# A graph kernel's Y blocks copied out of PSUM in units of two banks and one

## The reference, cut to what matters

```python
h = maximum(layernorm(x), 0)
x = x + gnn(h, src, dst)                  # layer 0: segment sum of gathered rows
h = maximum(layernorm(x), 0)
for l in range(2):                        # layers 1 and 2
    msg  = h[src]
    agg  = segment_sum(msg, dst * 65 + type)
    mean = agg / maximum(count, 1)
    conv = einsum('nrd,rdk->nk', mean, W[l]) + h @ root[l] + bias[l]
    h    = relu(conv) + relu(h @ res_W[l] + res_b[l])
x = x + h
```

## Time and profile before

| | us |
|---|---|
| median of 3 runs | 13232.2 (13220.0 to 13239.15) |
| the profiled execution | 13350.5 |
| its span, first to last instruction | 13348.7 |
| ScalarE busy in the span | 2265.7 (17%) |
| TensorE busy (matmuls) | 5052.4 (38%) |
| VectorE busy | 5562.3 (42%) |
| GpSimd busy | 8102.8 (61%) |

### The profile page before, as it was taken

One profiled execution on the slowest core, in us unless ns is written; L12 is line 12 of the kernel. 1 busy time (PEld: TensorE's weight loads), 2 busy tenths in 40 slices (PEclk: granted clock), 3 DMA queues, 4 the chain that ended last, 5 costly groups with the idle time before them and its releaser, 6 DMA issues.

```text
span 13348.7 us, 141317 instructions
## 1 busy us (share of the span) xinstructions
PE 5052.4 (38%) x38979; PEld 3570.3 (27%) x39273; DVE 5562.3 (42%) x20233; ACT 2265.7 (17%) x5671; POOL 8102.8 (61%) x8294
## 2 busy tenths in 40 slices
PE   3556566666633333333333333322222222222222
PEld 3434444444422222222222222211111111111111
DVE  6754444444446556556565555611111111111111
ACT  4733333333311111111111111100000000000000
POOL 7355545555546666666666666566666666666666
PEclk5677777777765656666565566655555555555555
DMA  2122222222233333333333333311111111111111
GB/s 73 38 69 91 87 86 90 91 91 86 94 117 118 121 116 123 117 122 118 121 115 116 123 123 116 128 24 24 24 24 24 24 24 24 24 24 24 24 24 32
DMA packets 485430, 1012.61 MB, mean 76 GB/s; under 512 B 191444, under 2 KB 237540, under 8 KB 484548
## 3 DMA queue, kind: packets, MB, share of 16 engines
q1 hardware_dynamic: 227204, 742.28, 15.0%
q0 software_dynamic: 257920, 266.40, 10.4%
HBM read 558.25 MB, written 453.13 MB: 76 GB/s over the span
## 4 chain that ended last, share of the span: by engine, by line
another core or an unknown queue 43%; DVE 30%; issue 13%; PE 11%; ACT 2%; DVEq 1%; DMA 1%; SPq 0%; ACTq 0%; POOL 0%; POOLq 0%
DVE w_raw L1504 9%; DVE onehot L1496 5%; DVE w_parts L1496 5%; PE y_ps L1137 4%; DVE same_more L1504 4%; PE block_ps L1224 3%; DVE ystage L1459 2%; ACT scr L936 1%; PE y_ps L1216 1%; PE sums_ps L1189 1%; DMA y_table<-ystage 1%; PE signs_ps L1216 0%; ACT ystage L926 0%; DVE w_room L1510 0%
## 5 line engine op out<-in xcount | busy, mean ns | idle before, releaser
L798 POOL DMA_INDIRECT rows<-y_table,idx_st x3234 | 3054.0, 944 | 1866.5 <-issue 1094.1
L798 POOL DMA_INDIRECT w_parts<-y_table,idx_st x3212 | 3032.3, 944 | 1691.8 <-issue 951.4
L798 POOL DMA_INDIRECT rows<-h_table,idx_st x1452 | 1685.9, 1161 | 1372.4 <-PE sums_ps L1189 703.8
L1565 DVE TENSOR_SCALAR rr<-rr 128x64 f32<-128x64 f32 x198 | 39.4, 199 | 4552.9 <-remote 4474.7
L1137 PE MATMUL y_ps<-scr,hT 128*128 128x512 bf16 (+1 forms) x2574 | 825.0, 477 | 1877.5 <-ACT ystage L926 1174.4
L1327 PE MATMUL sums_ps<-onehot,rows 128*64 128x64 f32 x6468 | 832.4, 293 | 1819.5 <-issue 1517.4
L902 ACT ACTIVATE idx_st<-edges 128x11 int32 (+1 forms) x720 | 141.6, 211 | 8114.7 <-remote 7518.2
L1327 PE MATMUL sums_ps<-w_parts 128*64 128x64 f32 x6424 | 814.8, 290 | 1712.8 <-issue 1479.5
L926 ACT ACTIVATE ystage<-y_ps 128x512 f32<-128x512 f32 (+1 forms) x1782 | 994.3, 567 | 1574.1 <-PE y_ps L1137 841.4
L1327 PEld LDWEIGHTS sums_ps<-onehot,rows 128*64 128x64 f32 x6468 | 706.1, 202 | 1961.7 <-issue 1666.1
L1327 PEld LDWEIGHTS sums_ps<-w_parts 128*64 128x64 f32 x6424 | 690.5, 199 | 1863.5 <-issue 1588.0
(11 more groups left out here) (226 smaller groups left out, 7203.2 us busy)
## 6 DMA issues: line engine op xcount, KB each, us to landing
y_table<-ystage SPq DMA_DIRECT2D x396, 768.0 KB
edges<-key_row SPq DMA_DIRECT2D x198, 832.0 KB
y_table<-ystage SPq DMA_DIRECT2D x198, 608.0 KB
w_raw<-key_row SPq DMA_DIRECT2D x99, 832.0 KB
rows<-y_table,idx_st POOLq DMA_INDIRECT x3234
w_parts<-y_table,idx_st POOLq DMA_INDIRECT x3212
rows<-h_table,idx_st POOLq DMA_INDIRECT x1452
rr<-y_table SPq DMA_DIRECT2D x198, 64.0 KB, 1.8
```

What stands on the lines that cost most here:

```text
L798: pool.indirect_dma_start(out=rows_of(l, u)[:, j, k, 0:D], out_offset=None, in_=table, in_offset=bass.IndirectOffsetOnAxis(ap=idx_of(l, u, ...
```

## The change

Two neighbouring chunks that lie in one group now share one copy. A block's nine chunks become six units: (c0, c1), (c2), (c3, c4), (c5), (c6, c7), (c8). The two-chunk units go to `y_pair`, the two banks of `y_ps` under one name; the one-chunk units go to the first bank of `count_pair`, the two banks of `signs_ps` and `deg_ps`. All counters count units: TensorE raises `y_done` after the last chunk of a unit, and waits only before the first chunk of a unit, for the copy of the unit before the last one. The stores are as before: three a block, with the same bytes.

```diff
+    UNITS = [(g, c, min(c + 2, g * SG + SG, YC)) for g in range(YG) for c in range(g * SG, min(g * SG + SG, YC), 2)]
+    YP = len(UNITS)
+    UNIT_OF = [p for p, (g, c0, c1) in enumerate(UNITS) for c in range(c0, c1)]
...
-        y_ps = [pb(f"y_ps{i}") for i in range(2)]
+        y_pair = ctx.enter_context(nc.psum_tensor("y_ps", [P, 2 * BANK], f32))
+        y_ps = [y_pair[:, i * BANK:(i + 1) * BANK] for i in range(2)]
...
-        signs_ps = pb("signs_ps")
-        deg_ps = pb("deg_ps")
+        count_pair = ctx.enter_context(nc.psum_tensor("signs_ps", [P, 2 * BANK], f32))
+        signs_ps, deg_ps = (count_pair[:, i * BANK:(i + 1) * BANK] for i in range(2))
+        y_pairs = [y_pair, count_pair]
...
-                    wait_alone(sp, y_read[l], s * YC + min(g * SG + SG, YC) + 1)
+                    wait_alone(sp, y_read[l], s * YP + UNIT_OF[min(g * SG + SG, YC) - 1] + 2)
...
-                    for c in range(g * SG, min(g * SG + SG, YC)):
-                        act.wait_ge(y_done[l], s * YC + c + 1)
-                        o = (c - g * SG) * BANK
-                        nc.scalar.activation(ystage[:, n % 2, o:o + y_cols(c)],
-                                             y_ps[c % 2][:, 0:y_cols(c)], ACT.Copy).then_inc(y_read[l], 1)
+                    for p, (_, c0, c1) in enumerate(UNITS):
+                        if UNITS[p][0] == g:
+                            act.wait_ge(y_done[l], s * YP + p + 1)
+                            o, w = (c0 - g * SG) * BANK, min(c1 * BANK, YW) - c0 * BANK
+                            nc.scalar.activation(ystage[:, n % 2, o:o + w], y_pairs[p % 2][:, 0:w], ACT.Copy)\
+                              .then_inc(y_read[l], 1)
...
-                pe.wait_ge(y_read[l], s * YC + max(c - 1, 0) + 1)
+                p = UNIT_OF[c]
+                at = c - UNITS[p][1]
+                if at == 0:
+                    pe.wait_ge(y_read[l], s * YP + max(p - 1, 0) + 1)
...
-                ins.then_inc(y_done[l], 1)
+                if c + 1 == UNITS[p][2]:
+                    ins.then_inc(y_done[l], 1)
```

More of the change, by code:

```diff
@@ L1129, in transform_chunk @@
             def transform_chunk(l, s, c, v=0):
-                pe.wait_ge(y_read[l], s * YC + max(c - 1, 0) + 1)
+                p = UNIT_OF[c]
+                at = c - UNITS[p][1]
+                if at == 0:
+                    pe.wait_ge(y_read[l], s * YP + max(p - 1, 0) + 1)
                 n = y_cols(c)
                 lastc = c == YC - 1
+                to = y_pairs[p % 2][:, at * BANK:at * BANK + n]
                 for a in range(3):
-                    ins = nc.tensor.matmul(y_ps[c % 2][:, 0:n], hT[:, v, a // 2, :],
-                                           parts_of[l][:, a, c * BANK:c * BANK + n],
+                    ins = nc.tensor.matmul(to, hT[:, v, a // 2, :], parts_of[l][:, a, c * BANK:c * BANK + n],
                                            start=a == 0, stop=a == 2 and not lastc)
@@ L1141, in transform_chunk @@
                     o = R * D - c * BANK
-                    ins = nc.tensor.matmul(y_ps[c % 2][:, o:o + 2 * D], ones[:, :], brow[:, D:3 * D],
-                                           start=False, stop=True)
-                ins.then_inc(y_done[l], 1)
+                    ins = nc.tensor.matmul(to[:, o:o + 2 * D], ones[:, :], brow[:, D:3 * D], start=False, stop=True)
+                if c + 1 == UNITS[p][2]:
+                    ins.then_inc(y_done[l], 1)
             def transform(l, s, parts=range(YG)):
@@ L1259, in pe_turn @@
                     else:
-                        pe.wait_ge(y_read[0], n * YC - YC + 1)
+                        pe.wait_ge(y_read[0], n * YP - YP + 1)
                     count_chunk(m, 0)
```

## The result

| | before | after |
|---|---|---|
| median, us | 13234.5 (13220.0 to 13239.2) | 13394.0 (13385.0 to 13411.1) |
| runs | 4 | 4 |
| time as a ratio | 1 | 1.0125 (95% interval 1.0112 to 1.0137) |
| the profiled execution | 13350.5 | 13411.1 |

The change makes the kernel 1.25% slower, by about 160 us. The prediction said 13194 us, faster. The profiled execution of the kernel before took 116 us longer than the median of four and that of the changed kernel 17 us, so their difference (61 us) is not that of the kernels. I therefore took a second profile of the kernel before (experiment 8). It took 13241 us, as its median, and what follows compares with it where I say so. The record doesn't name the chip of the first comparison; that of the second profile has a median of 13240 us where the first had 13234, so differences of stage lengths between them may carry some microseconds of the chips.

The account below looks back on a forecast made before the run. No engine is full; TensorE's Y waits in stage one, held notices within gather runs, were the ceiling at 174 us. Gains of 30 + 6 + 2 + 0 = 38 us take 13232 to 13194 us, range 13120 to 13265.

Parts of the forecast that it names:

- So 0: Stage two: c8 leaves the line and copies end 1.0 us sooner, but other work covers this, so no gain.
- if the held notices move to other places in the turn: One listed sign that the prediction is wrong; notices had only been replayed with their old times.
- D: Rival, stage two: the 1.0 us a step isn't covered, 138 us less in all, 13094 us; chance 0.06.
- Rival C: Slower: pairs make c3 and c6 wait longer; 13255 us, or 13287 with all stage-one blocks hit; chance 0.16.
- 0.43 us at c3 and c6: Each wait there is for a pair's copy, which ends up to 0.43 us later than the second single copy.
- The copies: ScalarE: a 1024-column copy takes 1.03 us; busy time falls by 101 us, covered by ScalarE's idle time.
- Stage one: The whole forecast gain lies here: 30 + 6 + 2 us, 38 us less.
- were to fall to 120: Stage one: TensorE's Y matmul waits fall from 174 to about 120 us.
- the ten blocks like the earlier trace: Stage-one blocks where c7 waits 3.66 us and c8 2.74 us; freeing them gives 30 us (17 to 50).
- 3 out of 1.7 to 5.0: Gain in us for each of those ten stage-one blocks, 3 taken from between 1.7 and 5.0.
- A (every held notice comes earlier): Rival, larger gain: with six notices a block, held ones come a period earlier; 74 us, 13158 us; chance 0.10.
- Stage three: It has no Y and stays at 4703 us.

Follow-up runs that it names:

- experiment 8: The kernel before, no edit, profiled a second time: 13241.4 us, its profiled execution 13241.6.
- experiment 3: The changed kernel, but in stage two c8 waits for the copy of (c6, c7): 13278.2 us, ratio 0.9972, on the chip with 13318.
- experiment 4: The kernel before, nine copies, but stage two's c8 in its own bank, free of c6's copy: ratio 1.0023 (chip with 13318), 1.0103 (chip with 13240).
- experiment 6: The changed kernel, but in stage two GpSimd waits for the copy of hT before the gathers of group 1: 13268.6 us, ratio 1.0032.
- experiment 5: The changed kernel, but in stage two each pair's first chunk also raises a semaphore on which nobody waits: 13382.0 us, ratio 1.0110.
- Experiments 2: The six units in one stage alone, the other as in the kernel before: stage one 13283.8 us, ratio 0.9973; stage two 13373.3 us, ratio 1.0037.

## Why the prediction was wrong

**The step that failed** is stage two, "So 0". It read two rows rightly, that GpSimd restarts on the indices and that TensorE's next sums wait 0.47 us for VectorE's matrices, and concluded that c8's 19.16 us wait covered nothing. For that one step this is so. But it is not the usual step: c8's wait is 12.3 us in the mean of that stage and 19.2 at most, and in the same profile j=0's sum follows the group of c8 with no idle in 45 of 95 steps (in 37 it waits 0.4 to 1.6 us for VectorE's matrices, in 13 about 1 us for nothing named). In the second profile it follows at once in all 95, and the latest matrices that VectorE had made were done 7.35 us earlier (median). In these steps c8 was the last thing that held the sum, and the sum's notice is what ScalarE's stage 0, and with it GpSimd's next indices, waits for. That path the prediction left out. With c8 free the sum begins, in half of the steps, before `stage 2` or beside it, stage 0 comes within 3.5 us, and the notices that are held next are those of j=1 and hT. The wait had kept an order. The prediction named the way in which it would be wrong, "if the held notices move to other places in the turn", for stage one, and it was in stage two that they moved. It gave a price only for a gain there (D, 100 us); the loss is 192. By experiments 3 and 4 it comes from c8's freedom, and by experiment 6 three quarters of it from GpSimd's 23rd gather before hT is copied.

**Rival C** ended on the right side by the wrong mechanism. Its 0.43 us at c3 and c6 are all there in experiment 3, which is faster than the kernel before. The Trainium skill's rule on rotating banks (Perfetto Trace Analysis, Optimizing Tensor Performance, Matmuls) doesn't decide either: experiment 4 has one bank a chunk and a third in the rotation, and loses 1.0%.

**The copies.** Right in size: a copy of 1024 columns takes 1.02 us (forecast 1.03). ScalarE is busy for 118 us less (2265.7 to 2147.3), or 115 against the second profile (2262.6), where 101 were forecast. As forecast, this is worth nothing by itself.

**Stage one.** Right in sign and, at the low end, in size: forecast 38 us with its own range from 15 up, measured 15 to 28 on the chips near 13235 (3055 and 3060 us without the units on one, 3032 to 3040 with them elsewhere), and 29 to 38 on that with 13318 (3082 and 3083 us with the units, 3112 and 3120 without). The Y matmuls' waits of 174 us, 136 in the second profile, were to fall to 120. They fell further, to 63 (50.4 for a copy, 12.3 that end as issue), but a new one of 67 us stands behind them. Waits of TensorE in stage one of the changed kernel, us, times, longest:

```profile
PE y_ps L1225 <- ACT ystage L932: 66.7, 10, 7.7
...
PE y_ps L1147 <- ACT ystage L932: 50.4, 42, 8.0
```

L1225 is the counting of the next turn. In the ten blocks like the earlier trace rows the 3.66 us before c7 and the 2.74 before c8 are gone, and instead the first counts wait 6.15 to 7.70 us each for the last copies. In the second profile of the kernel before these blocks wait once, 2.67 to 5.83 us (in one block twice, 5.67 together). The first and the ninth of the new waits, and c8 of the same blocks in that profile:

```profile
825.60 0.52 PE L1225 MATMUL y_ps<-w_room 64*128 64x99 bf16 x8 [6.38 <-ACT ystage L932]
2989.35 0.52 PE L1225 MATMUL y_ps<-w_room 64*128 64x99 bf16 x8 [6.33 <-ACT ystage L932]
```

```profile
824.76 0.66 PE L1137 MATMUL y_ps<-w_parts,hT 128*128 128x192 bf16 x3 [5.80 <-ACT ystage L926]
3004.11 0.66 PE L1137 MATMUL y_ps<-w_parts,hT 128*128 128x192 bf16 x3 [5.83 <-ACT ystage L926]
```

Eight periods take 2163.75 us and not 2179.35: 1.95 us each, where I had taken 3 out of 1.7 to 5.0; ten of them make the 20 us of the stage. I had expected a shorter wait there; it is as long as the two of the first profile together (6.40), so that the gain came out near the forecast is partly luck. A (every held notice comes earlier) did not happen.

**Stage three** was to stay, and did (4668 us, for 4670 in the second profile of the kernel before).

**What stays open.** Why the notice of j=1 passes alone when it is the first that is held, and together with hT's when j=0's stood before it; that these go together is counted above, and the number of notices is not the reason (experiment 5). When j=0's sum begins has a part in it: of the close steps in the four such profiles near 13235 (the changed kernel twice, experiments 4 and 5), those in which the sum began 0.5 us or more before `stage 2` were apart in 115 of 116, those in which it began less than 0.25 us before it, or later, in none of 21. Why on the chip with 13318 a close step is seldom an apart one with nine copies (3 of 72) and more often with six (22 of 55); there the early sums too are mostly not apart with nine copies (3 of 24 are). Why notices are held at all. What differs between the chips. Experiments 2 and 3, the two that beat the kernel before (by 0.27 and 0.28% with 13318, by 0.07 and 0.08%, within their intervals, with 10905), were not timed on a chip near 13235, where the change itself was; there stage one alone would give 15 to 28 us of 13235, an estimate from the stage lengths above.

## What to carry to other kernels

A long wait that "isn't what is late" may still keep an order. Before it is costed at nothing, ask what the freed engine does next, in which stretch of the busiest engine that falls, and who acts on it. Here it gave GpSimd its next indices too early, and the work that was left had no pause to run in. Take a second profile when the profiled execution is far from the median: of the 80 us that the first pair of profiles showed for stage one, 60 were gone with the second.

## What the runs showed of the hardware

- While GpSimd issues gathers back to back (one in 1.25 us), TensorE's notice on a semaphore can reach ScalarE 23.7 us late (j=1's sum, done 6046.36, acted on at 6070.04; 22.4 to 25.2 us over the 91 inner steps of that profile) and came 3 to 5 us into the next pause there; in half of the steps of the first profile it came 2 to 3 us into it. VectorE's notice to TensorE was held as well (3.9 us in the step shown of the changed kernel). In the first 6 us of such a run TensorE's notices came without delay (c0 to c5, 6070.66 to 6077.06).
- Held notices may come together (0.12 us apart) or singly (5.5 us apart), and in the changed kernel the steps are 49.3 or 53.7 us long by it; with GpSimd held until hT is copied the second sort takes 50.1 us (experiment 6).
- On two of five chips nothing was held (j=1's notice was acted on at most 0.13 us after the sum, in 95 steps of stage two in each kernel profiled there), and the same program took 10905 us and not 13235, 18% less, with gathers of the same 944 ns.
